# First attention block of a four-layer megakernel: where two DVE reads and one POOL step stand in the written-out order

## The reference, cut to what matters

```
q = rmsnorm(x @ Wq.T, qn);  k = rmsnorm(ctx @ Wk.T, kn);  v = ctx @ Wv.T
scores = q @ k.T / sqrt(128) + mask
out = softmax(scores) @ v
return out @ Wo.T
```

## Time and profile before

| what | value |
|---|---|
| median of three executions | 2335.64 us (2335.22 to 2337.76) |
| the profiled execution's own time | 2335.8 us |
| its span in the trace | 2334.0 us |
| PE busy | 2173.6 us (93% of the span), 14284 matmuls |
| DVE busy | 1322.0 us (57%) |
| ACT busy | 1146.0 us (49%) |
| POOL busy | 536.4 us (23%) |
| granted PE clock, mean | 0.981 of full speed |
| first attention block | about 58 to 620 us of the span |

### The profile page before, as it was taken

One profiled execution on the slowest core, in us unless ns is written; L12 is line 12 of the kernel. 1 busy time (PEld: TensorE's weight loads), 2 busy tenths in 40 slices (PEclk: granted clock), 3 DMA queues, 4 the chain that ended last, 5 costly groups with the idle time before them and its releaser, 6 DMA issues.

```text
span 2334.0 us, 40760 instructions
## 1 busy us (share of the span) xinstructions
PE 2173.6 (93%) x14284; PEld 1220.1 (52%) x14284; DVE 1322.0 (57%) x2695; ACT 1146.0 (49%) x3004; POOL 536.4 (23%) x936
## 2 busy tenths in 40 slices
PE   4799999999899899999999999998879899999998
PEld 2565555655554445555555555555434455555564
DVE  5566665666740556655656556555642455555654
ACT  4666666666412235554455544533322555666551
POOL 3332332322310312222122221212310222222221
PEclk9999999999989899999999999999979999999999
DMA  3110110110021112111111211101200111111000
GB/s 122 46 47 24 48 43 29 46 35 8 25 108 48 44 70 66 48 66 48 51 62 48 67 48 49 45 12 41 102 25 1 37 37 37 38 46 41 1 33 37
DMA packets 27366, 106.92 MB, mean 46 GB/s; under 512 B 4074, under 2 KB 12522, under 8 KB 17186
## 3 DMA queue, kind: packets, MB, share of 16 engines
q1 hardware_dynamic: 26722, 104.36, 12.7%
q10 hardware_dynamic: 448, 0.03, 0.0%
HBM read 102.29 MB, written 2.10 MB: 45 GB/s over the span
## 4 chain that ended last, share of the span: by engine, by line
PE 65%; DVE 14%; ACT 13%; issue 7%; POOL 1%; DMA 0%; ACTq 0%; DVEq 0%; POOLq 0%
PE bank L84 17%; PE bank L85 17%; PE bank L86 17%; ACT m_E L430 3%; PE bank L1788 3%; PE bank L1434 2%; PE bank L614 2%; DVE m_Sm L837 2%; ACT m_arena L311 2%; ACT m_arena L412 2%; DVE m_x L883 1%; DVE m_A L877 1%; PE bank L1334 1%; DVE m_nmax L854 1%; DVE m_arena L683 1%
## 5 line engine op out<-in xcount | busy, mean ns | idle before, releaser
L783 DVE TENSOR_TENSOR m_arena<-bank,m_arena 128x512 f16<-128x512 f32 x320 | 221.1, 691 | 507.2 <-ACT m_arena L412 505.3
L84 PE MATMUL bank<-m_input_parts,m_arena 128*128 128x512 f16 x1088 | 416.7, 383 | 8.4 <-DVE m_arena L783 2.3
L85 PE MATMUL bank<-m_input_parts,m_arena 128*128 128x512 f16 x1088 | 416.2, 383 | 0.0
L86 PE MATMUL bank<-m_input_parts,m_arena 128*128 128x512 f16 x1088 | 415.9, 382 | 0.0
L430 ACT ACTIVATE m_E<-m_Sm,m_nmax 128x64 f32<-128x64 f32 (+1 forms) x512 | 185.4, 363 | 386.5 <-DVE m_nmax L854 202.2
L895 POOL TENSOR_TENSOR m_E<-m_E,m_rinv 128x512 f32<-128x512 f32 (+1 forms) x192 | 172.5, 899 | 862.9 <-DVE m_rinv L868 862.9
L412 ACT ACTIVATE m_arena<-bank 128x512 f16<-128x512 f32 x320 | 189.7, 593 | 232.4 <-PE bank L86 231.9
L85 PE MATMUL bank<-m_wo_t,m_A 128*128 128x512 f16 x768 | 291.8, 380 | 0.0
L86 PE MATMUL bank<-m_wo_t,m_A 128*128 128x512 f16 x768 | 291.7, 380 | 0.0
L84 PE MATMUL bank<-m_wo_t,m_A 128*128 128x512 f16 x768 | 291.7, 380 | 0.0
L426 ACT ACTIVATE m_E<-bank,m_nmax,m_qk 128x128 f32<-128x128 f32 x256 | 113.8, 454 | 182.0 <-DVE m_nmax L825 182.0
(11 more groups left out here) (279 smaller groups left out, 4307.3 us busy)
## 6 DMA issues: line engine op xcount, KB each, us to landing
m_raw<-a_q SPq DMA_DIRECT2D x24, 1024.0 KB, 4.9
m_raw<-a_o SPq DMA_DIRECT2D x24, 1024.0 KB, 4.8
m_raw<-a_k SPq DMA_DIRECT2D x9, 1024.0 KB, 4.8
m_raw<-a_v SPq DMA_DIRECT2D x9, 1024.0 KB, 5.0
m_bias_in<-bias SPq DMA_DIRECT2D x64, 128.0 KB, 2.0
m_arena<-f_w SPq DMA_DIRECT2D x3, 1024.0 KB, 7.2
m_x<-x SPq DMA_DIRECT2D x2, 1024.0 KB, 7.0
m_arena<-ctx_t SPq DMA_DIRECT2D x4, 512.0 KB, 12.3
```

The lines of the kernel that those rows point to most:

```text
L84: pe.matmul(out, lhs[0], rhs[0], start=first, stop=False)
L85: pe.matmul(out, lhs[0], rhs[1], start=False, stop=False)
L86: return pe.matmul(out, lhs[1], rhs[0], start=False, stop=last)
L783: ins = dve.tensor_tensor(self.dest(name, part, 1), self.shaped(name, bank[m % 2][:, :]), self.dest(name, part, 0), ALU.subtract)
```

## The change

Three places of `events`, and the names under which DVE and POOL look for them. The DVE part of `q_sum` becomes an event of its own, `q_read`, which stands behind the scores of slots 2 and 6 and so ahead of `rinv` b. The POOL part of `k_rms` becomes `k_inv`, which stands at the head of the slot, ahead of `w_sum`. The DVE part of `k_rms` and the PE and POOL parts of `q_sum` stay where they were. No instruction is added or removed.

```diff
             if t == 8:
                 out.append(("f_norm", slot))
+            if normed == 2:
+                out.append(("k_inv", slot // 4))
             if made is not None:
                 out.append(("w_sum", made, misc))
                 misc += 1
...
                 out.append(("k_rms", slot // 4))
                 if ok(b):
                     out.append(("scores", b))
+                out.append(("q_read", misc, slot // 4))
             if normed == 3:
                 out.append(("k_turn", misc, slot // 4))
                 misc += 1
...
-                elif e[0] == "q_sum":
+                elif e[0] == "q_read":
                     _, misc, part = e
                     dve.wait_ge(*s["misc"].by(at(t, self.misc_per, self.NP + misc + 1)))
...
-                elif e[0] == "k_rms":
+                elif e[0] == "k_inv":
                     part = e[1]
                     pool.wait_ge(*s["k_tot"].by(at(t, 2, part + 1)))
                     pool.wait_ge(*s["k_n"].by(at(t, 2, part)))
```

## The result

| | before | changed |
|---|---|---|
| median of 20 executions | 2336.05 us (2330.89 to 2341.31) | 2332.02 us (2326.29 to 2334.51) |
| ratio, 95% interval | | 0.9980 (0.9972 to 0.9988) |
| a second set, other chip time | 2334.59 us (24 executions) | 2329.41 us (11), 0.9984 (0.9975 to 0.9993) |
| last half's L794 (L797 now) after the second half's | 495.49 us | 491.10 us |

By the medians the change is worth 4.0 us; 4.7 were forecast. The ratio is not the quotient of the two medians; by it the gain is 4.7 us here and 3.7 in the second set.

What follows compares the result with a forecast made beforehand. The block was taken as bound by a chain of DVE and ACT, PE only nearly as long. Six k slots 1.9, six v slots 2.0, period 7's third slot 0.35, last 0.2: 4.7 us, 2335.6 to 2330.9; range 2328.5 to 2338.5.

Steps and rivals of the forecast that it cites:

- second rival: PE in the attention block: it gains all of its 20.5 us wait for the query sums, 2315.1 us; chance 0.05.
- The read's place costs nothing: DVE reads the sums while idle 1.50 us before L868; the 0.42 pair runs from about 1.75 to 2.2, free.
- Everything behind L868 moves one for one: DVE, if PE's sums no longer end before 2.5: the cover goes and all behind L868 is delayed equally.
- v slots: Seventh slots, handling a v slab: L837 starts 0.34 us sooner; six give 2.0 us, the first counted at 0.2.
- k slots: Third slots handling a k slab: 0.42 less 0.11 leaves 0.31 us each, six give 1.9; bounds 0.1 and 0.6.
- the last factor ends at 4.87, covered by 0.1: POOL in k slab slots: pushed-back factors end at 4.87, before DVE's L683 needs them at 4.95; thinnest cover.
- The rule of the 0.55: DVE and POOL in k slab slots: the product of E holds L683, which ends 0.55 us behind that product.
- The queries' power against L683: POOL's queries' power (2.91 us), now starting 0.37 before L683 in v slab slots, was taken not to block it.
- first rival: Queries' power holds L683 for its whole length in v slab slots: 9.4 us slower, 2345.0; chance 0.12.
- the half hold: Half of the power's inputs fetched ahead: L683 held some 1.3 us, about 2337 us; chance 0.13 for something between.
- I am wrong if halves get shorter by more than 0.5: Sign against the forecast, per half of the attention block: a half shortened by over 0.5 us.
- The third rival: Reads move, but covers thinner than 0.1 (last factor before L683) or later DVE waits on ACT lose the gain: 2335.6; chance 0.07.

Runs made afterwards that it cites:

- reads only: Kernel before with only DVE's read of the query sums moved, POOL's key step left behind the slab factors: 2328.92 us, ratio 0.9973, stretch 489.60 us.
- Reads too early: Changed kernel with DVE's read of the sums one event earlier, ahead of the scores of b: 2364.23 us, 1.0124 of the kernel before, stretch 520.74 us.
- Key step only: Kernel before with only POOL's key step moved, DVE's read left at the end of the slot: 2337.34 us, ratio 1.0008, stretch 496.30 us.
- all low parts late: Reads-moved kernel with DVE's low slab parts of slots 2, 3, 6, 7 put in the next slot: 2326.93 us, 0.9962 of the kernel before, stretch 488.24.

## Why the prediction was right, and where a term was off

- **What bounds the block: right.** The wait of 20.5 us was not to be had. It moved to the scores, as said: 1.01 in the k slot shown against "about 1 us". The second rival (2315.1) is refuted.
- **The read's place costs nothing: right, with a wrong term.** L868 (L871 now) stays at 2.94 in every half but the last. The copy was forecast as part of a pair of 0.42 and took 0.69, because POOL's key product now runs at that time (with the product back in its place, in "reads only", it takes 0.17); it ends at 2.63, 0.3 before the cover ends. "Reads too early" shows what it costs without cover. "Everything behind L868 moves one for one" was too strict by 0.2: in the last half PE's sums come late and L871 stands at 3.16, but the next instruction waits for ACT until 3.20 in any case, and the next scores start as early as in the half before (4.96 and 4.95).
- **v slots: right.** 0.34 forecast, 0.35 measured; in the first of them, counted at 0.2, it was 0.33, and in the last half, also counted at 0.2, 0.34.
- **k slots: mis-sized.** 0.31 forecast; 0.18 in three of the six and 0.16 or 0.17 in the others, 1.0 us in place of 1.9 (1.2 by the lengths of the halves). The step that failed is "the last factor ends at 4.87, covered by 0.1". I had taken the key step's length from the earlier trace rows, period 7, where its product ends at 2.43. Inside the hardware loop it ends at 2.60 or 2.51: in the third slot shown above its power starts at 0.38, and 0.17 idle follow. So the last factor ends at 5.02, L686 starts at 5.12 instead of 4.95, the product of E ends at 5.58, and L686 ends 0.55 behind that, at 6.13. The rule of the 0.55 held exactly; its input did not.
- **The queries' power against L683: right.** In v slots it starts 0.31 before L686, which takes 0.74 as alone. In k slots it comes behind the waiting L686 and is itself held (3.35 instead of 2.90), which costs nothing. In the first v slot it comes behind L686, too, and takes 3.35. The first rival (2345.0) is refuted, and the half hold with it.
- **The sum: close in part by luck.** Without the last half, which the stretch does not hold, 4.45 were forecast, and the stretch is 4.4 us shorter. By the lengths of the halves the six k slots gave 1.2 instead of 1.9, the first v slot 0.35 instead of 0.2, the other six 2.5 instead of 2.0, and the third slot of period 7 0.37 for 0.35. The medians say 4.0, in the second set 5.2.
- **A sign that came though the case held.** "I am wrong if halves get shorter by more than 0.5": the half behind which the loop turns over for the second time got shorter by 0.54 (0.59 in the second trace), the first such by 0.45. Some 0.25 us of the total lies there beyond the 0.36 of the other v slots. "Key step only", too, has 0.18 in the second one, where its other v slots have nothing. No run says why.
- **The third rival** named exactly the cover that was too thin, and priced it too high: it took 0.7 to 0.9 us, not all.

One thing of the totals needs the clock, which is granted at full (2.4 GHz) or half level (1.2 GHz); the rows give the mean. In the trace of the changed kernel the last half starts 5.7 us earlier than before (4.4 of them in the stretch, the rest ahead of it), yet the span is only 1.3 us shorter. Two windows of the trace before (us, busy time of PE, PEld, DVE, ACT and POOL with their instructions, then PEclk, the granted clock, DMA share and GB/s):

```profile
600.00:700.00 100.00, 91.04 (x431) 52.00 (x432) 63.93 (x144) 24.88 (x76) 22.92 (x27) 0.91 0.21 77
1600.00:1740.00 140.00, 109.00 (x508) 60.39 (x507) 78.86 (x161) 44.16 (x96) 34.53 (x59) 0.88 0.19 68
```

the same windows of the changed kernel's trace:

```profile
600.00:700.00 100.00, 91.15 (x403) 51.80 (x404) 60.11 (x133) 23.21 (x68) 22.52 (x26) 0.88 0.17 67
1600.00:1740.00 140.00, 109.35 (x478) 59.54 (x477) 77.91 (x158) 43.76 (x95) 33.53 (x58) 0.85 0.18 67
```

and of its second trace, whose span is 2324.6 us:

```profile
600.00:700.00 100.00, 91.19 (x426) 51.92 (x423) 63.26 (x139) 24.44 (x72) 23.32 (x27) 0.93 0.19 72
1600.00:1740.00 140.00, 110.80 (x494) 59.55 (x495) 76.64 (x153) 42.38 (x88) 32.41 (x57) 0.89 0.15 58
```

The same kernel was granted 0.88 in one trace and 0.93 in the other for 600 to 700 us, and 0.85 and 0.89 for 1600 to 1740 us; the kernel before had 0.91 and 0.88. Against before, the changed kernel's trace is granted 0.03 less over 100 us and over 140 us, which is worth some 7 us at the full clock, and 0.01 more from 700 to 1000 us (0.97 against 0.96), some 3 us: by this rough estimate, from means rounded to 0.01, the clock behind the block takes about 4 us, and 4.4 are missing. PE was busy for 91 of the 100 us and for 109 to 111 of the 140; no run tells what set the level there. The two traces of the changed kernel agree to 0.03 us in the stretch inside the block while their spans differ by 8.1. So in one execution more than in another the clock hides or adds to what the block gives. That the spread of the other executions' times has the same source fits this and is not shown.

## What to carry to other kernels

A wait on the busiest engine names who came last, not what is gained by bringing it forward: follow the next stop of that engine as well, and if it starts right behind a chain of other engines, only what shortens that chain counts. A blocking read belongs where its engine would stand idle for another reason, and what it leaves behind in the chain is all that is won. Of the two edits here one carried the gain and the other cost a part of it; moving a step ahead of others on an engine is only free when the last of those others is covered by more than the rows themselves differ between the hardware loop and the written-out periods. Add up the parts as well as the total: here 0.7 us too little in one kind of slot met 0.6 us too much in the other.

## What the runs showed of the hardware

- A DVE instruction with two inputs in SBUF and a POOL product from SBUF held each other up, in both directions: the large low part of 2048 columns (L692 of "all low parts late") held a key product to 3.14 us (1.04 alone), and the product of E held L686 to 1.01 (0.74 alone). A DVE copy from SBUF to SBUF of only 16 columns was held by the key product as well (0.60 to 0.85, alone 0.17).
- The Trainium skill (SBUF — State Buffer, "SBUF: two separate sides") says that the one that starts first keeps the shared ports for the whole instruction. The runs agree for the long streaming operations, where 0.1 us in who comes first turned the roles ("all low parts late"), and for the copy. They disagree for POOL's power on 128x16: it had been running for 0.31 of its 2.90 us when L686 started, and L686 took 0.74; over all the traces it had run for 0.15 to 2.06 us at that point, and the low part never took more than 0.75. When L686 was there first, the power was held (3.35 us). That it fetches its few inputs at once and then only computes was argued, not tested.
- The same two POOL operations (power and product of the key) ended 0.08 to 0.17 us later, counted from L797, inside the hardware loop than in the written-out periods, at equal durations: the pause between them is 0.16 or 0.17 instead of 0.08, and in the third slot of every second period the power also starts 0.08 later. That the semaphore values are computed from a register there may be the reason; it wasn't tried.
